# Two elementwise passes of the last node update moved from GpSimd to VectorE

## The chip, the cores and the metric

The kernel runs on one core of a Trainium2 chip. The metric is the device time of one execution in microseconds; three executions of the kernel before are shown, and the middle one is taken. A second, profiled execution gives the trace from which all rows below come. PE is the matrix engine TensorE, DVE the VectorE, ACT the ScalarE, POOL the GpSimd, SP the engine that issues plain transfers.

## The reference

The program is a four-layer graph network on 50000 nodes of 64 channels and 25000 edges. Every layer adds something to the residual `x` and then norms `x` again. The stage that the change touches finishes the third layer. For every node:

```
t = layernorm(h + attended @ Wo' + bias)          (without gain and offset)
y = layernorm(t * g1 + gelu(t @ W1' + b1') @ W2 + bias)
x = x + y * g2 + b2                               (g2, b2: gain and offset of the second norm)
h = relu(layernorm(x));  out starts as x + h
```

`attended` holds one row per edge; the row of a node's last edge is the one that it needs, so it is gathered by an index per node. The last line prepares the fourth layer: its first term is `h`, and `x + h` is written to `out`, to which the later terms are added.

## The kernel before

`node_update(layer 2)` walks over 14 super-tiles. A super-tile is 128 partitions x 28 nodes x 64 channels (a tile of 128x1792 f32 in the profile) and is cut in 7 parts of 4 nodes. Tiles alternate between two buffers each: `A` (gathered rows), `Z` (`h` of before), `T`, `Y`, `TG`, `X` (the residual), `H` (the new `h`). The order on each engine is written out by hand, and they meet through counting semaphores. Super-tile d goes through:

- POOL, `gather` (L1742): 28 indirect DMAs, one per node column, four to a part. Then, when `T` is ready, `gained` (L1722): `TG = T * g1`.
- PE, `attend(d)`: for each part two transposes of `A` (L1327), a bias product (L1333) and two products (L1353). ACT copies the transposes out of PSUM (L1427). The transposes of part i+1 stand ahead of the products of part i. A transposition waits for its part's four gathers; the products of a part wait until DVE has evacuated the part two before.
- PE, `mlp(d)`: turns `T`, two products up (L1368), GELU on ACT (L1433), four products down (L1379). PE's order is attend(d+1), mlp(d), attend(d+2), and so on.
- DVE, `evacuate`: after each part's products it adds PSUM to `Z` (L1554, attend) or to `TG` (L1556, mlp). Between the evacuations it does the norms of up to three super-tiles: during attend(d) the relu and scaling of super-tile d-3 (`H`, L1539) at part 0, the scaling of `T` of d-1 at part 1 (L1540), the centring of `Y` of d-2 at part 2 (L1527) and its variance at part 5 (L1531). During mlp it does the scaling, gain (L1667), sum with the residual (L1671), the totals, centrings and variances. Each of these passes over a whole super-tile.
- ACT also squares the centred rows (L1438) and takes roots (L1442), in a fixed order with its copies.
- POOL, `offset` (L1728): `X = X + b2`, after `X` has been loaded. POOL, `tail` (L1734): `X = X + H`, after `H` is there. It releases SP.
- SP, `swap_x`: waits for the tail, stores `H` and `X`, waits until the store of `X` has landed and loads the next `X` into the same buffer.

POOL's order in the middle of the stage is gathers(d+2), offset(d), gained(d+1), tail(d-1), gathers(d+3): three passes between two sets of gathers. Below, G(d) is the time at which POOL ends the last gather of super-tile d.

Of the kernel before, what the change touches and what calls it, by code (L numbers as in the profile page):

```python
# [1141 lines left out]
def node_update(nc, net, layer, sums=None):  # L1142
# [19 lines left out]
    with ExitStack() as ctx:  # L1162
# [44 lines left out]
        if layer == 2:  # L1207
            Y = [sb(f"y{s}", [P, G, C]) for s in range(2)]
            TG = [sb(f"tg{s}", [P, G, C]) for s in range(2)]
            node_end = sb("node_end", [P, SUPER, G])  # L1210
            ends_loaded = sem("ends_loaded")
            u = [sb(f"u{b}", [FF, 2, CH // 2]) for b in range(2)]

            pf = [ctx.enter_context(nc.psum_tensor(f"{n}pf{b}", [P, 2, 512], F32)) for b in range(2)]
            loaded_x = [sem(f"loaded_x{s}") for s in range(2)]
            gathered = [[sem(f"gathered{s}_{i}") for i in range(SUBS)] for s in range(2)]
            up_done, gelu_done, t_ready, tg_ready, xa_ready, tail_ready = map(
                sem, ("up_done", "gelu_done", "t_ready", "tg_ready", "xa_ready", "tail_ready"))
        weight = (net.w_upd, net.w_lin, net.w_out)[layer]
        x_in = (net.x_in, net.x1, net.x2)[layer]  # L1220
        h_in = (net.h0, net.h1d, net.h2)[layer]
# [21 lines left out]
        with nc.Block() as block:  # L1243
# [268 lines left out]
            def _(v):  # L1512
# [16 lines left out]
                def variance(r, n=0):  # L1529
                    v.wait_ge(squared[n], r + 1)  # L1530
                    nc.vector.tensor_reduce(rstd[n][:, :], SQ[n][:, :, :], AX.X, ALU.add).then_inc(var_ready[n], 1)  # L1531
# [93 lines left out]
                else:  # L1625
                    def attend(c, phase, x=None, t=None, y=None):

                        for i in range(SUBS):
                            if c is not None:
                                if i == 0:  # L1630
                                    v.wait_ge(loaded[c[1]], 16 * in_loads * (c[2] + 1))
                                evacuate(c, phase, i, 0)
                            if x is not None and i == 0:
                                v.wait_ge(stored_h[x[1]], 16 * x[2])
                                nc.vector.tensor_copy(H[x[1]][:, :, C:C + 1], node_end[:, bass.ds(x[0], 1), :].rearrange("p n g -> p g n"))
                                scale(H[x[1]][:, :, 0:C], 2 * x[0] + 1, 1, relu=True).then_inc(normed, 1)
                            elif t is not None and i == 1:
                                scale(T[t[1]][:, :, :], t[0]).then_inc(t_ready, 1)
                            elif y is not None and i == 2:
                                centre(Y[y[1]][:, :, :], 1)  # L1640
                            elif y is not None and i == 5:
                                variance(2 * y[0], 1)
                        v.drain()
                        if c is not None:
                            v.sem_inc(inputs_used, 1)

                    def mlp(c, phase, t=None, y=None):

                        for i in range(SUBS):
                            if c is not None:  # L1650
                                if i == 0:
                                    v.wait_ge(tg_ready, c[0] + 1)
                                evacuate(c, phase, i, 1)
                            if t is not None:
                                if i == 0:
                                    total(T[t[1]][:, :, :])
                                elif i == 1:
                                    centre(T[t[1]][:, :, :])
                                elif i == 3:
                                    variance(t[0])  # L1660
                            if y is not None:
                                xs, ys = X[y[1]][:, :, :], Y[y[1]][:, :, :]
                                if i == 0:
                                    scale(ys, 2 * y[0], 1)
                                elif i == 1:
                                    v.drain()
                                    nc.vector.tensor_tensor(ys, ys, channels(net.norms[:, 2, :]), ALU.mult)  # L1667
                                elif i == 2:
                                    v.drain()
                                    v.wait_ge(xa_ready, y[0] + 1)  # L1670
                                    nc.vector.tensor_tensor(xs, xs, ys, ALU.add)  # L1671
                                elif i == 3:
                                    v.drain()
                                    total(xs, 1)
                                elif i == 4:
                                    centre(xs, 1)
                                elif i == 5:
                                    variance(2 * y[0] + 1, 1)
                        v.drain()
                        if c is not None:  # L1680
                            total(Y[c[1]][:, :, :], 1)
# [19 lines left out]
            @block.gpsimd  # L1701
            def _(pool):
                if layer < 2:
                    with pool.Fori(0, SUPER // 2) as t:
                        for s in range(2):
                            pool.wait_ge(loaded[s], 16 * in_loads * (t + 1))
                            if layer == 0:
                                pool.wait_ge(deg_ready, 2 * t + s + 1)
                                nc.gpsimd.tensor_tensor(Z[s][:, :, C:P], summed(2 * t + s),  # L1709
                                                        inv_count[s][:, :].unsqueeze(2).to_broadcast([P, G, C]), ALU.mult).then_inc(z_ready, 1)  # L1710
                            else:
                                nc.gpsimd.tensor_tensor(A[s][:, :, :], summed(2 * t + s), Z[s][:, :, C:C + 1].to_broadcast([P, G, C]), ALU.mult)
                                pool.drain()
                                nc.gpsimd.tensor_tensor(A[s][:, :, :], A[s][:, :, :], Z[s][:, :, 0:C], ALU.add).then_inc(z_ready, 1)
                else:
                    def channels(which):
                        return net.norms[:, which, :].unsqueeze(1).to_broadcast([P, G, C])

                    def gained(c):

                        pool.wait_ge(t_ready, c[0] + 1)
                        nc.gpsimd.tensor_tensor(TG[c[1]][:, :, :], T[c[1]][:, :, :], channels(0), ALU.mult).then_inc(tg_ready, 1)  # L1722

                    def offset(c):

                        number, s, h = c
                        pool.wait_ge(loaded_x[s], 16 * (h + 1))
                        nc.gpsimd.tensor_tensor(X[s][:, :, :], X[s][:, :, :], channels(3), ALU.add).then_inc(xa_ready, 1)  # L1728

                    def tail(c):  # L1730

                        number, s, h = c
                        pool.wait_ge(normed, number + 1)
                        nc.gpsimd.tensor_tensor(X[s][:, :, :], X[s][:, :, :], H[s][:, :, 0:C], ALU.add).then_inc(tail_ready, 1)  # L1734

                    def gather(c):
                        number, s, h = c
                        if h > 0:
                            pool.wait_ge(inputs_used, number - 1)
                        for j in range(G):  # L1740
                            tile = G * number + j
                            pool.indirect_dma_start(A[s][:, j, :], None, net.attended[:, :],  # L1742
                                                    bass.IndirectOffsetOnAxis(ap=net.dst_end[:, tile:tile + 1], axis=0)).then_inc(gathered[s][j // J], 16)
                    gather(at(0, 0))
                    gather(at(0, 1))
                    for d in range(2):
                        offset(at(0, d))
                        gained(at(0, d))
                        gather(at(0, d + 2))
                    for d in range(2, SUPER):  # L1750
                        gained(at(0, d))
                        tail(at(0, d - 2))
                        if d + 2 < SUPER:
                            gather(at(0, d + 2))
                        offset(at(0, d))
                    tail(at(0, LAST - 1))
                    tail(at(0, LAST))


SET = 4  # L1760
# [844 lines left out]
```

## Time and profile before

| | us |
|---|---|
| median of three executions (5319.16 to 5332.62) | 5328.72 |
| the profiled execution | 5317.69 |
| its span, first to last instruction | 5315.9 |
| the last node update, of that span | 3035 to 3915 |
| busy over the span: PE, DVE, POOL, ACT | 3389.1, 2638.3, 3086.2, 1088.7 |

The engines run side by side, so busy times do not add up to the span. The stages of the program are separated by barriers; a microsecond won inside the last node update is a microsecond of the whole. The busy shares over the span therefore say little about this stage, which is read by stretches of its own.

### The profile page before, as it was taken

What the parts mean: (1) busy time and instruction counts of PE and PEld (TensorE: products, weight loads), DVE (VectorE), ACT (ScalarE), POOL (GpSimd) and SP (SyncE); (2) the same over time, 40 slices, a digit from 0 to 9 for tenths busy, and PEclk for the clock granted to TensorE, in tenths of its full rate; (3) what the DMA queues carried; (4) which work ended last, traced back from release to release, by engine and by line L of the source; (5) the groups of instructions that cost most, each with busy time, mean ns of one, the idle gap of its engine ahead of it and who ended that gap; (6) DMA issues with size and microseconds to landing.
All of it is one profiled execution on the core that took longest, in us unless ns stands there. A gap on an engine that the chain in (4) does not pass through costs nothing. (4 is left out here: it accounts for less than half of the span.)

```text
span 5315.9 us, 58056 instructions
## 1 busy us (share of the span) xinstructions
PE 3389.1 (64%) x12064; PEld 2038.0 (38%) x12064; DVE 2638.3 (50%) x6534; ACT 1088.7 (20%) x2025; POOL 3086.2 (58%) x2552
## 2 busy tenths in 40 slices
PE   3654735555896788676898677776635555555524
PEld 1222534444675666452333244554412222222213
DVE  5997741111355322465666546666644444444423
ACT  0232411111122111122333223332311111111100
POOL 0374048887111881335676588888538888787740
PEclk7686655555555555555555555555557777777765
DMA  3122621111464110451111323333212222233210
GB/s 140 44 71 68 269 102 22 23 23 20 105 166 124 23 22 6 160 203 49 34 34 35 58 42 73 84 86 72 70 43 30 30 30 30 27 30 30 27 16 3
DMA packets 360442, 335.42 MB, mean 63 GB/s; under 512 B 268311, under 2 KB 297481, under 8 KB 360292
## 3 DMA queue, kind: packets, MB, share of 16 engines
q1 hardware_dynamic: 232910, 253.30, 15.1%
q0 software_dynamic: 114032, 67.92, 11.9%
q10 hardware_dynamic: 13350, 12.40, 0.7%
q8 instruction: 69, 1.13, 0.1%
q14 instruction: 81, 0.66, 0.0%
HBM read 172.92 MB, written 162.66 MB: 63 GB/s over the span
## 5 line engine op out<-in xcount | busy, mean ns | idle before, releaser
L843 PE MATMUL e_ps<-e_msg,e_hot 128*128 x2408 | 598.0, 425 | 325.8 <-POOL e_msg L754 231.4
L843 PEld LDWEIGHTS e_ps<-e_msg,e_hot 128*128 128x128 f32 x2408 | 539.4, 326 | 430.5 <-issue 430.5
L2269 POOL DMA_INDIRECT out<-d_out,d_end x356 | 592.0, 1663 | 172.1 <-issue 167.2
L1742 POOL DMA_INDIRECT u_a<-attended,dst_end x392 | 501.0, 1278 | 149.0 <-issue 117.4
L2313 PE MATMUL d_pl<-d_hot,d_fields 128*65 128x512 f32 x712 | 503.1, 872 | 0.0
L815 DVE TENSOR_TENSOR e_ps<-e_ps,e_before 128x65 f32<-128x65 f32 (+1 forms) x172 | 40.1, 233 | 792.5 <-PE e_ps L843 792.5
L2032 POOL DMA_INDIRECT list<-s_rec,s_place x200 | 199.3, 996 | 288.9 <-DVE s_place L1948 232.8
L735 POOL DMA_INDIRECT e_msg<-from_src,e_src x200 | 194.1, 970 | 286.3 <-DMA e_first<-lot_first 231.8
L1427 ACT ACTIVATE u_zt<-u_pt 128x256 f32<-128x256 f32 (+1 forms) x392 | 163.5, 433 | 615.6 <-PE u_pt L1327 615.4
L946 POOL DMA_INDIRECT a_ends<-h,a_src x200 | 201.5, 1007 | 146.7 <-DMA a_etype<-in_etype 93.7
L740 POOL DMA_INDIRECT e_msg<-h1d,e_src x200 | 221.4, 1107 | 102.7 <-issue 54.8
L2294 PE MATMUL d_pc<-d_liveb,d_before 128*128 128x4 bf16 x89 | 14.6, 165 | 387.2 <-DVE d_prod L2411 387.2
L2313 PEld LDWEIGHTS d_pl<-d_hot,d_fields 128*65 128x65 f32 x712 | 140.7, 213 | 292.5 <-issue 292.5
L788 ACT ACTIVATE sums<-e_ps 128x455 f32 (+1 forms) x172 | 94.2, 548 | 748.5 <-DVE e_ps L815 748.5
L737 POOL DMA_INDIRECT e_near<-from_dst,e_dst x200 | 209.4, 1047 | 61.0 <-issue 61.0
L2305 PE MATMUL d_pr<-ident,d_scan 65*128 65x65 f32 x356 | 63.9, 334 | 279.0 <-DVE d_scan L2434 279.0
L1327 PE MATMUL u_pt<-ident,u_a 128*128 128x128 f32 x392 | 118.7, 420 | 191.9 <-DMA u_a<-attended,dst_end 174.4
L946 POOL DMA_INDIRECT a_ends<-h,a_dst x200 | 202.2, 1011 | 66.6 <-issue 66.0
L2261 POOL DMA_INDIRECT d_near<-term,d_rec x196 | 189.9, 969 | 85.1 <-issue 71.1
L1709 POOL TENSOR_TENSOR u_z<-sums,u_inv_count 128x1792 f32<-128x1792 f32 x14 | 44.6, 3189 | 306.7 <-DVE u_inv_count L1563 261.2
L1333 PE MATMUL u_po<-bias_parts,ones 3*128 3x256 bf16 x392 | 149.8, 382 | 111.9 <-ACT u_zt L1427 80.5
L2261 POOL DMA_INDIRECT d_near<-terms,d_rec_idx x168 | 163.5, 973 | 98.5 <-DMA d_rec_w<-list_w 49.8
(370 smaller groups left out, 7910.4 us busy)
## 6 DMA issues: line engine op xcount, KB each, us to landing
u_z<-h SPq DMA_DIRECT2D x28, 896.0 KB, 6.3
x<-sums SPq DMA_DIRECT2D x28, 896.0 KB, 7.8
u_x<-x SPq DMA_DIRECT2D x28, 896.0 KB, 7.4
terms<-s_zeros SPq DMA_DIRECT2D x16, 812.5 KB
s_key_row<-src_key SPq DMA_DIRECT2D x50, 256.0 KB, 3.0
h1d<-u_h SPq DMA_DIRECT2D x14, 910.0 KB, 9.5
u_z<-h1d SPq DMA_DIRECT2D x14, 910.0 KB, 4.6
term<-u_h SPq DMA_DIRECT2D x14, 910.0 KB, 3.6
```

The lines of the kernel that those rows point to most:

```text
L735: pool.indirect_dma_start(msg[:, b, 0:C], None, net.from_src[:, :], bass.IndirectOffsetOnAxis(ap=src[:, b:b + 1], axis=0)).then_inc(gather ...
L737: pool.indirect_dma_start(near[c % 3][:, j, :], None, net.from_dst[:, :], bass.IndirectOffsetOnAxis(ap=dst[:, b:b + 1], axis=0)).then_inc( ...
L740: pool.indirect_dma_start(msg[:, b, :], None, net.h1d[:, :], bass.IndirectOffsetOnAxis(ap=src[:, b:b + 1], axis=0)).then_inc(gathered[c % ...
L843: last = nc.tensor.matmul(to, hot[s][:, q, :], rows, start=False, stop=q == LOT - 1)
L946: pool.indirect_dma_start(ends[s][:, j, half * C:(half + 1) * C], None, net.h2[:, :], bass.IndirectOffsetOnAxis(ap=rows, axis=0)).then_inc ...
L1333: nc.tensor.matmul(po[b][:, 0:J * C], net.ones3[:, :], net.bias_parts[:, which, :, :].rearrange("k j c -> k (j c)"), start=True, stop=False)
L1427: nc.scalar.activation(zt[b][:, :], pt[b][:, 0:TURNS * P], ACT.Copy).then_inc(zt_ready, 1)
L1742: pool.indirect_dma_start(A[s][:, j, :], None, net.attended[:, :], bass.IndirectOffsetOnAxis(ap=net.dst_end[:, tile:tile + 1], axis=0)).th ...
L2032: pool.indirect_dma_start(net.lists0[:, :], bass.IndirectOffsetOnAxis(ap=place[:, t:t + 1], axis=0), rec[:, t, :], None).then_inc(scattere ...
L2261: pool.indirect_dma_start(near[s][:, j, :], None, table[:, :], bass.IndirectOffsetOnAxis(ap=row, axis=0)).then_inc(gathered[s], 16)
L2269: pool.indirect_dma_start(net.out[:, :], bass.IndirectOffsetOnAxis(ap=end[s][:, j:j + 1], axis=0), out[s][:, j, 0:C], None, bounds_check=N ...
L2313: last = nc.tensor.matmul(pl[0:WEIGHT + 1, :], fields[:, j, :], hot[:, j, :], start=j == 0, stop=j == J - 1)
```

## The change

`X + b2` and `X + H` are issued by DVE in `attend` instead of by POOL. The first stands behind the evacuation of part 3 and belongs to super-tile d-2; it waits for the load of `X`, and what follows on DVE waits with it. The second stands behind the evacuation of part 4, belongs to super-tile d-3, and has a drain ahead of it; it sends the signal for SP's stores. POOL's `offset` and `tail` go with the semaphore between them and the sum with the residual, so that POOL's order becomes gathers(d+2), gained(d+1), gathers(d+3). Nothing else of the program differs.

```diff
--- before.py
+++ after.py
@@ -1214,8 +1214,8 @@
             pf = [ctx.enter_context(nc.psum_tensor(f"{n}pf{b}", [P, 2, 512], F32)) for b in range(2)]
             loaded_x = [sem(f"loaded_x{s}") for s in range(2)]
             gathered = [[sem(f"gathered{s}_{i}") for i in range(SUBS)] for s in range(2)]
-            up_done, gelu_done, t_ready, tg_ready, xa_ready, tail_ready = map(
-                sem, ("up_done", "gelu_done", "t_ready", "tg_ready", "xa_ready", "tail_ready"))
+            up_done, gelu_done, t_ready, tg_ready, tail_ready = map(
+                sem, ("up_done", "gelu_done", "t_ready", "tg_ready", "tail_ready"))
         weight = (net.w_upd, net.w_lin, net.w_out)[layer]
         x_in = (net.x_in, net.x1, net.x2)[layer]
         h_in = (net.h0, net.h1d, net.h2)[layer]
@@ -1640,6 +1640,12 @@
                                 centre(Y[y[1]][:, :, :], 1)
                             elif y is not None and i == 5:
                                 variance(2 * y[0], 1)
+                            if y is not None and i == 3:
+                                v.wait_ge(loaded_x[y[1]], 16 * (y[2] + 1))
+                                nc.vector.tensor_tensor(X[y[1]][:, :, :], X[y[1]][:, :, :], channels(net.norms[:, 3, :]), ALU.add)
+                            elif x is not None and i == 4:
+                                v.drain()
+                                nc.vector.tensor_tensor(X[x[1]][:, :, :], X[x[1]][:, :, :], H[x[1]][:, :, 0:C], ALU.add).then_inc(tail_ready, 1)
                         v.drain()
                         if c is not None:
                             v.sem_inc(inputs_used, 1)
@@ -1667,7 +1673,6 @@
                                     nc.vector.tensor_tensor(ys, ys, channels(net.norms[:, 2, :]), ALU.mult)
                                 elif i == 2:
                                     v.drain()
-                                    v.wait_ge(xa_ready, y[0] + 1)
                                     nc.vector.tensor_tensor(xs, xs, ys, ALU.add)
                                 elif i == 3:
                                     v.drain()
@@ -1721,18 +1726,6 @@
                         pool.wait_ge(t_ready, c[0] + 1)
                         nc.gpsimd.tensor_tensor(TG[c[1]][:, :, :], T[c[1]][:, :, :], channels(0), ALU.mult).then_inc(tg_ready, 1)
 
-                    def offset(c):
-
-                        number, s, h = c
-                        pool.wait_ge(loaded_x[s], 16 * (h + 1))
-                        nc.gpsimd.tensor_tensor(X[s][:, :, :], X[s][:, :, :], channels(3), ALU.add).then_inc(xa_ready, 1)
-
-                    def tail(c):
-
-                        number, s, h = c
-                        pool.wait_ge(normed, number + 1)
-                        nc.gpsimd.tensor_tensor(X[s][:, :, :], X[s][:, :, :], H[s][:, :, 0:C], ALU.add).then_inc(tail_ready, 1)
-
                     def gather(c):
                         number, s, h = c
                         if h > 0:
@@ -1743,18 +1736,10 @@
                                                     bass.IndirectOffsetOnAxis(ap=net.dst_end[:, tile:tile + 1], axis=0)).then_inc(gathered[s][j // J], 16)
                     gather(at(0, 0))
                     gather(at(0, 1))
-                    for d in range(2):
-                        offset(at(0, d))
+                    for d in range(SUPER):
                         gained(at(0, d))
-                        gather(at(0, d + 2))
-                    for d in range(2, SUPER):
-                        gained(at(0, d))
-                        tail(at(0, d - 2))
                         if d + 2 < SUPER:
                             gather(at(0, d + 2))
-                        offset(at(0, d))
-                    tail(at(0, LAST - 1))
-                    tail(at(0, LAST))
 
 
 SET = 4

```

## Rows read from the trace of the kernel before

**Rows 1.** Windows of the last node update: lead-in, one early period, nine periods, drain.
```profile
...
core 0: us, PE busy (x) PEld busy (x) DVE busy (x) ACT busy (x) POOL busy (x), PEclk, DMA share, GB/s
3035.00:3155.70 120.70, 67.29 (x240) 44.59 (x240) 32.35 (x41) 23.89 (x42) 95.52 (x87) 0.50 0.43 70
...
3209.50:3263.30 53.80, 41.26 (x154) 28.53 (x154) 35.11 (x35) 17.55 (x29) 45.40 (x31) 0.50 0.39 86
3263.30:3780.40 517.10, 373.44 (x1386) 256.36 (x1386) 315.91 (x315) 158.13 (x261) 441.45 (x281) 0.50 0.36 78
3780.40:3915.40 135.00, 58.67 (x222) 40.59 (x222) 89.80 (x64) 30.94 (x46) 34.42 (x9) 0.50 0.18 69
...
```

**Rows 2.** Waits of PE, POOL, SP from 3324 to 3738 us: total, times, longest.
```profile
...
PE u_pt L1327 <- DMA u_a<-attended,dst_end: 75.6, 21, 6.1
...
POOL u_a L1742 <- issue: 59.5, 199, 0.3
...
SPq L1254 <- DMA out<-u_x: 46.0, 7, 7.0
...
```

**Rows 3.** Timeline of POOL, one period; start, duration, operation, idle before.
```profile
...
3435.80 3.97 POOL L1728 TENSOR_TENSOR u_x<-u_x,norms 128x1792 f32<-128x1792 f32 x1
...
3447.45 0.97 POOL L1742 DMA_INDIRECT u_a<-attended,dst_end  x1 [0.16 <-issue]
...
3453.86 2.62 POOL L1742 DMA_INDIRECT u_a<-attended,dst_end  x1 [0.31 <-issue]
3456.78 1.81 POOL L1742 DMA_INDIRECT u_a<-attended,dst_end  x1 [0.30 <-issue]
...
3462.59 0.94 POOL L1742 DMA_INDIRECT u_a<-attended,dst_end  x1 [0.30 <-issue]
...
3492.20 0.94 POOL L1742 DMA_INDIRECT u_a<-attended,dst_end  x1 [0.30 <-issue]
...
```

**Rows 4.** Groups by line, 3324 to 3738 us: POOL's gathers and two passes, mean ns.
```profile
...
L1742 POOL DMA_INDIRECT u_a<-attended,dst_end x199 | 265.6, 1335 | 59.5 <-issue 59.5
...
L1728 POOL TENSOR_TENSOR u_x<-u_x,norms 128x1792 f32<-128x1792 f32 x8 | 31.8, 3973 | 0.1
...
L1734 POOL TENSOR_TENSOR u_x<-u_x,u_h 128x1792 f32<-128x1792 f32 x8 | 29.3, 3658 | 0.0
...
```

**Rows 5.** Timeline of DVE, the same period.
```profile
...
3453.63 2.03 DVE L1527 TENSOR_TENSOR u_xc<-u_t,u_mean 128x1792 f32<-128x1792 f32 x1
3455.75 2.03 DVE L1667 TENSOR_TENSOR u_y<-u_y,norms 128x1792 f32<-128x1792 f32 x1
...
3462.24 2.01 DVE L1531 TENSOR_REDUCE u_rstd<-u_sq 128x28 f32<-128x1792 f32 x1
...
3484.76 0.42 DVE L1554 TENSOR_TENSOR u_t<-u_po,u_z 128x256 f32<-128x256 f32 x1
3492.46 0.42 DVE L1554 TENSOR_TENSOR u_t<-u_po,u_z 128x256 f32<-128x256 f32 x1 [7.28 <-PE u_po L1353]
```

**Rows 6.** Timeline of PE, the same period: two transposes that follow the gathers.
```profile
...
3437.81 0.66 PE L1327 MATMUL u_pt<-ident,u_a 128*128 128x128 f32 x2 [2.69 <-DMA u_a<-attended,dst_end]
...
3490.29 0.66 PE L1327 MATMUL u_pt<-ident,u_a 128*128 128x128 f32 x2 [6.10 <-DMA u_a<-attended,dst_end]
...
```

**Rows 7.** Timeline of DVE in the drain.
```profile
...
3803.22 5.29 DVE L1671 TENSOR_TENSOR u_x<-u_x,u_y 128x1792 f32<-128x1792 f32 x1
...
3831.78 5.37 DVE L1527 TENSOR_TENSOR u_xc<-u_y,u_mean 128x1792 f32<-128x1792 f32 x1
3838.91 2.02 DVE L1531 TENSOR_REDUCE u_rstd<-u_sq 128x28 f32<-128x1792 f32 x1 [1.76 <-ACT u_sq L1438]
...
```

**Rows 8.** Timeline of POOL in the drain.
```profile
...
3802.48 4.14 POOL L1728 TENSOR_TENSOR u_x<-u_x,norms 128x1792 f32<-128x1792 f32 x1 [10.61 <-DMA u_x<-x]
...
3902.99 3.64 POOL L1734 TENSOR_TENSOR u_x<-u_x,u_h 128x1792 f32<-128x1792 f32 x1 [24.13 <-DVE u_h L1539]
```

**Rows 9.** DMA issues on the page: size and us to landing.
```profile
...
u_x<-x SPq DMA_DIRECT2D x28, 896.0 KB, 7.4
...
```

## The prediction

> **What bounds the kernel now.** I first cut the stage into windows [rows 1]. From 3263.3 to 3780.4 us it repeats nine times with a period of 517.1/9 = 57.5 us; the period before those takes 53.8 us, since POOL makes only two passes in it. PE is busy for 373.4/9 = 41.5 us of a period and DVE for 35.1 us; neither is full. Next come the waits [rows 2]: POOL never waits for another engine, only "issue" stands ahead of its gathers (0.30 us each), so POOL is full. PE waits for gathers 75.6 us in 414 us, which is 10.5 us per period. So POOL's chain sets the period, and PE, with its other waits in, would need 57.5 - 10.5 = 47.0 us. The granted clock is 0.50 (1.2 GHz) in every window, and PE's own speed does not matter as long as it waits for gathers.
>
> The timeline of POOL [rows 3] shows what fills it. Call G the end of the last gather: 3435.8, and again 3492.20 + 0.94 = 3493.14. From G three passes take 11.65 us (to 3447.45), and then 28 gathers follow. A gather takes 0.94 us plus 0.30, but the mean is 1.335 us [rows 4]: (1.335 - 0.944) x 28 = 10.9 us per period is stretch. The timeline of DVE [rows 5] tells where it comes from. A pass with two inputs in SBUF starts at 3453.63 and ends at 3455.66; the gather of 3453.86 ends at 3456.48, 0.82 us later [rows 3]. The next such pass (3455.75 to 3457.78) catches the gather of 3456.78 for its last microsecond and it takes 1.81 us. The reduction of 3462.24, one input, leaves the gather of 3462.59 at 0.94. Eight gathers of a period are stretched, and DVE makes eight passes with two SBUF inputs in gather time. My rule for the sum: a gather that starts while such a pass runs ends 0.82 us after the pass. Replayed over the eight passes it gives 11.65 + 34.7 + 11.0 = 57.4 us, the measured period.
>
> **The change, part by part.** *Taken off POOL:* 3.97 us and 3.66 us per period [rows 4]. On the chain one pass of 4.1 us (with 0.16 us of issue) stays of 11.65: -7.6 us per period.
>
> *Put on DVE, first pass (`X + b2`).* It has the shape and kind of the passes in [rows 5], so it takes 2.03 us. It stands behind the evacuation of part 3, which starts at 3484.76, 49.0 us behind G [rows 5]; the pass runs from +49.5 to +51.5. PE's place relative to G stays as it is: its last transposition of `A` starts 2.0 us behind G, when that gather has landed [rows 6], and from there to part 3 of the next attend it did not depend on how late POOL was. The pass lies in gather time, so it stretches a gather. Bounds: 0.87 us (the 1.81 us gather) and 2.03 us (the whole pass). By the rule it catches the 28th gather, which ends at 51.53 + 0.82 = 52.35 instead of 51.1: +1.2 us.
>
> *Second pass (`X + H`), 2.03 us.* The evacuation of part 4 starts at 3492.46 and ends at 3492.88 [rows 5], 2.2 us behind the transposition of 3490.29 that followed a gather [rows 6], and 0.26 us ahead of G. With a drain the pass starts just ahead of G, and `gained`, which now starts right behind G, meets it. What happens when POOL's and DVE's passes meet is seen in the drain: DVE's pass of 3803.22 takes 5.29 us, because POOL's had started at 3802.48 [rows 7, 8]; the second to come waits out the first. Here POOL loses the rest of DVE's pass, 1.8 us. If POOL is first, DVE waits 4 us and then catches the first gather, for about as much. Bounds again 0.87 and 2.03; I take 1.8. What is queued behind either pass on DVE is the evacuation of parts 4 and 5, and PE waits for those. The cover is the 7.28 us that DVE idles ahead of part 4 [rows 5] and the 10.5 us of PE; without cover it is 4.1 us of DVE time per period.
>
> *Sum of a period.* The eight old passes fall on other gathers by this shift and cost 10.6 instead of 11.0. From G: 4.1 + 1.8 + 34.7 + 10.6 + 1.2 = 52.4 us, -5.1 us.
>
> *SP.* The signal for the stores now comes near G and not three passes later; the store of `X` holds SP up to 7.0 us [rows 2], the load lands in 7.4 us [rows 9], and the first pass wants it some 49 us on. Cost nothing; if that cover went, DVE would stand in the wait with all evacuations behind it. The removed semaphore costs nothing.
>
> *Lead-in.* Up to G(3), POOL loses two passes `X + b2` (-7.9). The first one on DVE comes behind a G that is now 4 us earlier, so it waits for `gained` and catches a gather (+1.9), the other stretches one (+1.3): -4.7 us.
>
> *From G(3) to G(13).* One period 53.8 to 52.4, -1.4; nine from 57.5 to 52.4, 517.1 - 9 x 52.35 = -45.9.
>
> *Drain.* The 5.29 us pass no longer meets POOL's: 3.3 us of DVE, of which PE sees between none and all; I take 1.3, since DVE has idle time behind it. The pass of 3831.78 (5.37) loses 3.3 us behind POOL's `X + H`; now two passes of 2.1 us stand behind it instead, but the 1.76 us wait for ACT's square [rows 7] is hidden by them: -0.9. The same shape once more for the last super-tile: -1.0. The very last pass, 3.64 us on POOL [rows 8], becomes a drain and 2.03 on DVE: -1.6. Together -4.8.
>
> Sum: -4.7 - 1.4 - 45.9 - 4.8 = **-57 us**. Against the profiled execution (5317.7) this is 5261; the median of the runs shown is 11 us above that execution, and I predict for it 5328.7 - 57 = 5272.
>
> The stretched gather is where row and notes part. The Trainium skill (SBUF — State Buffer, "Who interferes with whom") says that a DVE instruction with two SBUF inputs contends only with a GpSimd instruction that reads SBUF, and adds as an inference that such a pass did not stall DMAs whose descriptors GpSimd makes. Taken to the letter the two passes would cost POOL nothing, which is the second case below. The trace speaks against it by the gather of 2.62 us [rows 3].
>
> **The rivals.** *POOL is relieved in full.* The added passes fall where they catch no gather and no pass. Period 57.5 - 7.6 = 49.9 us, still above PE's 47.0; 9 x 7.6 + 3.9 + 7.9 + 4.8 = -85, 5244 us. Against it: eight of eight such passes are stretched for now. Chance 0.07.
>
> *DVE and PE take over.* In attend the evacuations of parts 0 to 3 already have passes between them, and now parts 3 and 4 too. If the `X + H` pass always loses to `gained` and waits its 3.97 us, and all of this reaches PE, its loop is 47.0 + 4.1 + 4.0 = 55.1 us. Gain 2.4 us in nine periods, a loss of 1.3 in the early one, lead-in and drain as above: about -30, 5299 us. For it: the 5.37 us pass [rows 7]. Against it: the idle 7.28 us just there. Chance 0.14.
>
> *Nothing left.* Catches of 2.03 us at both passes and an attend that is slower than I see, 57 us per period: within 16 us of before. Chance 0.05.
>
> *Slower: both passes lose the port.* The place is attend, parts 3 to 5; each pass waits 3.97 us for a pass of POOL, and PE waits for both: 47.0 + 2 x (2.03 + 3.97) = 59.0 us, +1.5 in nine periods and +5.2 in the early one: some +19, 5348 us. It decides once more than 10.5 us reach PE in a period. Against it: only one POOL pass is left per period for the two to meet. Chance 0.03.
>
> That the passes are not moved at all is excluded by the diff.
>
> **How the numbers follow.** My forecast has 0.71: 5272, with both added passes at 0.87 us (period about 51.2) 5261, with both at 2.03 us (about 53.5) 5283; executions differ by some 7 us around that. The measurement can tell about 0.3%, 16 us, from no change. Range for 8 in 10: 5252 to 5293; it reaches toward the full relief and toward the takeover by DVE, without holding either. Faster by over 0.3%: 0.71 + 0.07 + 0.14 = 0.92, taken down to 0.91; within: 0.06; slower: 0.03.
>
> **What would show it.** Right: windows of the same nine periods sum to about 471 us; POOL still waits for nobody; ten gathers or passes of POOL are stretched per period, one of them `gained` with nearly 5.8 us instead of 3.97; the gathers' mean in a period stays near 1.36 us; PE's wait for gathers falls to some 5 us per period; DVE is busy for 39 us of 52. The DVE passes in attend take 2.03 us. Wrong: POOL waits for `T` or for used inputs (then PE or DVE sets the period), the `X + H` pass takes 5 to 6 us and PE waits for evacuations, or the gathers' mean falls to what eight passes make.

## The result and the profile after

Five executions of the changed kernel have a median of 5279.1 us (5256.0 to 5281.7), five of the kernel before 5320.4 us. The ratio is 0.991, with an interval of 0.9893 to 0.9926: 48 us gained (39 to 57). The two medians differ by 41.3 us; the changed kernel's executions lie in two groups, 5256 to 5259 and 5279 to 5282 us. The forecast was 5272 us, -57.

The profiled execution, the fastest of the five, took 5256.0 us with a span of 5254.2, which is 61.7 us less than before. Not all of that is the change. The last node update starts its first gather at 3018.39 us instead of 3034.83, though no code ahead of it differs, and the stage behind it is 4.8 us longer. The stage itself, from its first gather to the first instruction of the next, takes 834.7 us instead of 884.7: **-50.0 us**. In what follows I compare this stage, whose steady periods repeat within 0.2 us, and not the whole.

Windows of the changed kernel, cut at G(3), G(4) and G(13) as in [rows 1], and last a window of one period:

```profile
...
core 0: us, PE busy (x) PEld busy (x) DVE busy (x) ACT busy (x) POOL busy (x), PEclk, DMA share, GB/s
3018.39:3186.60 168.21, 103.84 (x394) 70.11 (x394) 69.21 (x77) 40.66 (x71) 134.64 (x114) 0.52 0.38 62
3186.60:3237.67 51.07, 39.83 (x151) 27.72 (x151) 40.46 (x35) 16.70 (x29) 42.67 (x30) 0.50 0.42 90
3237.67:3708.45 470.78, 354.79 (x1366) 247.94 (x1367) 375.39 (x329) 157.13 (x259) 358.37 (x261) 0.53 0.40 86
3708.45:3853.10 144.65, 65.09 (x247) 45.25 (x246) 102.72 (x81) 33.68 (x50) 7.92 (x2) 0.50 0.17 64
3448.96:3501.77 52.81, 39.61 (x153) 27.93 (x154) 42.20 (x38) 17.17 (x28) 39.82 (x29) 0.53 0.41 87
...
```

The nine periods sum to 470.8 us; 471 was forecast. DVE has 375.4 us in them instead of 315.9, POOL 358.4 instead of 441.5: POOL is no longer full. The waits, over the eight last periods, from 3290.52 to 3713.04 us (line waited for, total, times, longest):

```profile
...
PE u_po L1333 <- issue: 40.8, 11, 5.1
PE u_pf L1368 <- ACT u_zt L1427: 35.8, 16, 2.7
PE u_po L1333 <- ACT u_u L1433: 18.3, 8, 2.3
PE u_po L1333 <- DVE u_t L1554: 6.0, 8, 0.8
...
```

```profile
...
POOL u_a L1735 <- issue: 66.0, 217, 0.3
POOL u_tg L1727 <- DVE u_t L1540: 37.0, 8, 4.6
```

PE's wait for gathers [rows 2] is gone altogether. POOL now waits for `T` once per period, 4.6 us each. PE's largest wait is put down to "issue", up to 5.1 us. Its cause is in the timelines. POOL's, of one period:

```profile
...
3443.40 0.94 POOL L1735 DMA_INDIRECT u_a<-attended,dst_end  x1 [0.30 <-issue]
3448.96 3.96 POOL L1727 TENSOR_TENSOR u_tg<-u_t,norms 128x1792 f32<-128x1792 f32 x1 [4.62 <-DVE u_t L1540]
3453.07 0.97 POOL L1735 DMA_INDIRECT u_a<-attended,dst_end  x1
3454.34 1.61 POOL L1735 DMA_INDIRECT u_a<-attended,dst_end  x1 [0.30 <-issue]
3456.26 1.95 POOL L1735 DMA_INDIRECT u_a<-attended,dst_end  x1 [0.31 <-issue]
3458.51 2.14 POOL L1735 DMA_INDIRECT u_a<-attended,dst_end  x1 [0.30 <-issue]
```

The gathers of a super-tile end at 3444.34 and POOL stands until `T` is scaled. DVE's timeline around it:

```profile
...
3446.85 2.03 DVE L1540 TENSOR_TENSOR u_t<-u_xc,u_rstd 128x1792 f32<-128x1792 f32 x1
3448.79 0.42 DVE L1554 TENSOR_TENSOR u_t<-u_po,u_z 128x256 f32<-128x256 f32 x1
3449.30 3.65 DVE L1525 TENSOR_SCALAR u_mean<-u_mean 128x28 f32<-128x28 f32 x1
3453.03 2.10 DVE L1527 TENSOR_TENSOR u_xc<-u_y,u_mean 128x1792 f32<-128x1792 f32 x1
3455.05 0.41 DVE L1554 TENSOR_TENSOR u_t<-u_po,u_z 128x256 f32<-128x256 f32 x1
3455.38 2.01 DVE L1645 TENSOR_TENSOR u_x<-u_x,norms 128x1792 f32<-128x1792 f32 x1
...
3457.81 2.03 DVE L1648 TENSOR_TENSOR u_x<-u_x,u_h 128x1792 f32<-128x1792 f32 x1
...
3467.82 0.42 DVE L1556 TENSOR_TENSOR u_y<-u_po,u_tg 128x256 f32<-128x256 f32 x1 [5.39 <-PE u_po L1379]
...
3499.66 2.03 DVE L1540 TENSOR_TENSOR u_t<-u_xc,u_rstd 128x1792 f32<-128x1792 f32 x1
...
```

The scaling of `T` ends at 3448.88 and POOL's pass starts at 3448.96. On DVE the evacuation of part 2 goes through in its usual 0.42 us, and behind it comes a scaling of 28 means per partition, which took 0.18 to 0.39 us in the periods before. It takes 3.65 us now: it stands until POOL's pass ends at 3452.92. From 3446.85 to 3460 DVE has no gap. From one scaling of `T` to the next it is 3499.66 - 3446.85 = 52.81 us, against 57.5 before. PE feels it:

```profile
...
3444.01 1.22 PE L1353 MATMUL u_po<-w_out,u_zt 128*128 128x128 f32 x4
...
3446.86 0.71 PE L1353 MATMUL u_po<-w_out,u_zt 128*128 128x128 f32 x4
...
3455.56 0.37 PE L1333 MATMUL u_po<-bias_parts,ones 3*128 3x256 bf16 x1 [5.12 <-issue]
...
3457.82 0.37 PE L1333 MATMUL u_po<-bias_parts,ones 3*128 3x256 bf16 x1 [0.75 <-DVE u_t L1554]
...
3462.87 2.08 PE L1368 MATMUL u_pf<-u_zt,w 64*128 64x256 f32 x8 [2.67 <-ACT u_zt L1427]
...
```

PE's products of part 5 start at 3455.56, when DVE has evacuated part 3 at 3455.46; the wait of 5.12 us is DVE's lateness. The wait of 2.67 us at the start of mlp has the same source, by way of ACT:

```profile
...
3462.13 0.32 ACT L1442 ACTIVATE u_rstd<-u_rstd,eps 128x28 f32<-128x28 f32 x1 [5.01 <-DVE u_rstd L1531]
3462.36 0.64 ACT L1427 ACTIVATE u_zt<-u_pt 128x256 f32<-128x256 f32 x2
...
```

In ACT's fixed order the root of `Y`'s variance stands ahead of the copies of `T`'s transposes, and it waits for the variance that DVE makes behind part 5.

In the drain, the pass that took 5.29 us [rows 7] is down to 2.03, the means' scaling stands behind POOL's pass as it did before the change, and the last pass of the stage is on DVE with 2.02 us instead of 3.64 [rows 8]:

```profile
...
3741.77 2.03 DVE L1676 TENSOR_TENSOR u_x<-u_x,u_y 128x1792 f32<-128x1792 f32 x1
...
3764.78 3.98 DVE L1525 TENSOR_SCALAR u_mean<-u_mean 128x28 f32<-128x28 f32 x1
...
3837.51 2.02 DVE L1648 TENSOR_TENSOR u_x<-u_x,u_h 128x1792 f32<-128x1792 f32 x1
...
```

### The profile page after: what moved, and what is told of

It reads as the page before. It is cut to its first block and busy times, and to the rows that moved or that the text cites. A ratio compares the mean times of both kernels' runs of the same rounds, so it can differ in the third digit from the quotient of the medians.

```text
span 5254.2 us, 58073 instructions
## 1 busy us (share of the span) xinstructions
PE 3366.0 (64%) x12064; PEld 2026.4 (39%) x12064; DVE 2716.5 (52%) x6562; ACT 1088.7 (21%) x2025; POOL 2973.1 (57%) x2524
## 5 line engine op out<-in xcount | busy, mean ns | idle before, releaser
L1735 POOL DMA_INDIRECT u_a<-attended,dst_end x392 | 488.1, 1245 | 149.5 <-issue 116.3
L2393 DVE SCALAR_TENSOR_TENSOR d_live<-d_near,d_inside 128x4 f32<-128x4 f32 x89 | 14.5, 163 | 392.0 <-DMA d_near<-term,d_rec 222.5
```

## Experiments

The period below is from one scaling of `T` to the next in the middle of the stage; the stage runs from its first gather to the first instruction of the next stage; the time is of the profiled execution, or a median where several were timed. A single time is not compared below; the period is.

| kernel | period, us | POOL's wait for T per period | stage, us | time, us |
|---|---|---|---|---|
| before | 57.44 | none | 884.7 | 5320.4 |
| the change | 52.82 | 4.62 | 834.7 | 5279.1 |
| gain_behind_4_gathers | 52.2 | none | 823.8 | 5265.1 |
| gain_on_dve | 49.52 | (no pass on POOL) | 790.5 | 5239.2 |
| gain_on_dve_again | 49.52 | (no pass on POOL) | 786.5 | 5239.7 |
| only_b2_on_dve | 55.40 | none | 865.3 | 5303.7 |
| no_x_passes | 49.9 | none | 794.5 | 5227.1 |
| before_plus_two_input_pass | 58.45 | none | 898.8 | 5319.2 |
| before_plus_reduction | 57.44 | none | 884.4 | 5310.5 |
| after_plus_reduction | 54.75 | 5.87 | 857.2 | 5285.7 |
| b2_behind_part_6 | 51.0 | 2.0 | disturbed | 5426.9 |
| x_h_only_on_dve | 56.0 to 56.9 | 5.12 | disturbed | 5464.9 |
| gain_on_dve_b2_behind_part_6 | 47.6 | (no pass on POOL) | disturbed | 5427.1 |
| gain_b2_part_6_again | 47.5 to 50.0, mean 48.9 | (no pass on POOL) | 776.6 | 5224.1 |

The three marked as disturbed ran on a chip on which the kernel before took 5682 us; only their steady periods are used.

**What does a DVE pass cost POOL?** The kernel before, with one more operation behind part 3 of attend:

```diff
                                 evacuate(c, phase, i, 0)
+                                if i == 3:
+                                    nc.vector.tensor_tensor(spare[:, :, :], Z[c[1]][:, :, :], channels(net.norms[:, 3, :]), ALU.add)
```

> The kernel before, with one more DVE pass of two SBUF inputs (Z + b2 into a buffer that nobody reads) behind the evacuation of part 3 of attend. Theory: POOL sets the period, the pass stretches one gather and nothing else, +0.9 to +2.0 us on 57.4 us, 1.2 us by the rule (a caught gather ends 0.82 us after the pass), so 58.6 us. Rival, a DVE pass costs nothing while POOL is the bound, since the gathers' long ones come from elsewhere: 57.4 us.

and with `nc.vector.tensor_reduce(spare[:, :, 0], Z[c[1]][:, :, :], AX.X, ALU.add)` in its place:

> The kernel before, with a DVE reduction over Z (one SBUF input, 2.0 us) in the same place. Theory: a pass with one input doesn't stretch a gather, 57.4 us. Rival, any DVE pass of 2 us stretches a gather: 58.6 us as with two inputs.

The groups of gathers on the two pages, first with two inputs, then with the reduction:

```profile
...
L1745 POOL DMA_INDIRECT u_a<-attended,dst_end x392 | 514.9, 1314 | 147.6 <-issue 117.4
...
```

```profile
...
L1745 POOL DMA_INDIRECT u_a<-attended,dst_end x392 | 500.6, 1277 | 149.4 <-issue 117.4
...
```

Two inputs: 58.45 us, +1.0; the mean gather is longer by 0.037 us, which times 28 is the same 1.0. The reduction: 57.44 us, nothing. The stretched gather is shown: while POOL is full, a DVE pass with two SBUF inputs costs its period 1.0 us at this place (1.2 by my rule), and this reduction with a single input is free.

**Who sets the period of the changed kernel?** The same reduction, free for POOL, in the changed kernel:

> The changed kernel with the same reduction of 2.0 us (one input, which by the theory costs POOL nothing) behind part 3 of attend. Theory: in the changed kernel DVE's chain through attend sets the period, so the 2.0 us are seen in full: 52.8 to 54.8 us, stage 834.7 + 9 x 2 = 853 us. Rival, POOL's gathers set it: 52.8 us, 834 us.

The period rises from 52.82 to 54.75 us, by nearly all of its 2.0 us, and POOL waits 5.87 us for `T` instead of 4.62; its gathers take up the other 0.7 us (waits of POOL, 3290 to 3690 us):

```profile
...
POOL u_tg L1730 <- DVE u_t L1541: 47.0, 8, 5.9
```

So DVE's chain through attend sets the period, not POOL.

**Is the blocked scaling part of it?** POOL's pass with `g1` behind the first gathers of the next super-tile:

```diff
                     for d in range(SUPER):
+                        if d + 2 < SUPER:
+                            gather(at(0, d + 2), 0, 4)
                         gained(at(0, d))
                         if d + 2 < SUPER:
-                            gather(at(0, d + 2))
+                            gather(at(0, d + 2), 4, G)
```

> The changed kernel, but POOL issues the first four gathers of the next super-tile ahead of its pass with g1. The stage is counted from its first gather to the first instruction of the next stage: 884.7 us before, 834.7 us with the change. Theory: a loop through attend on DVE and PE now sets the period of 52.8 us, and 3.3 us of it is the small scaling of Y's mean, which waits behind POOL's pass because both start when T is ready. With the pass behind four gathers the scaling should take 0.4 us again, the loop 49.4 us, and POOL (34.7 us of gathers, 4.1 us for its pass, ten stretched gathers of 1.2 us) sets the period at 50.8 to 51.5 us: stage 820 to 825 us. Rival 1: POOL's gathers set the period as before and the wait for T is only slack; then the order on POOL changes nothing, 834 us. Rival 2: the added passes on DVE alone set it; then the scaling may be short but the period stays 52.8 us.

Groups by line and the wait of PE for gathers, 3290 to 3680 us:

```profile
...
L1735 POOL DMA_INDIRECT u_a<-attended,dst_end x211 | 300.5, 1424 | 63.3 <-issue 63.3
...
L1525 DVE TENSOR_SCALAR u_mean<-u_mean 128x28 f32<-128x28 f32 x22 | 7.1, 325 | 2.1
...
```

```profile
...
PE u_pt L1327 <- DMA u_a<-attended,dst_end: 49.1, 8, 6.6
...
```

The means' scaling is back at a mean of 0.33 us (its three uses in a period of the changed kernel take 3.65, 0.39 and 0.18 us), PE waits for gathers again, and POOL waits for nobody. POOL took over at 52.2 us, above the 51.5 that I had stated, since ten catches cost (1.424 - 0.944) x 28 = 13.4 us and not the 12 that I had put in. The block is gone, and the period gains little because POOL, full again, needs 52.2 us. In the whole time the gain cannot be told from the change's: a ratio of 0.9906 (0.9887 to 0.9924) to before. How long DVE's loop is without the block had to be seen where POOL has no pass at all:

```diff
+                            if t is not None and i == 6:
+                                nc.vector.tensor_tensor(TG[t[1]][:, :, :], T[t[1]][:, :, :], channels(net.norms[:, 0, :]), ALU.mult).then_inc(tg_ready, 1)
```

```diff
                     for d in range(SUPER):
-                        gained(at(0, d))
                         if d + 2 < SUPER:
```

> The changed kernel with the last pass of POOL (T times g1) on DVE too, behind part 6 of attend, so that POOL has gathers alone. Theory: the loop through DVE loses the 3.3 us wait and gains a pass of 2.03 us, 52.8 - 3.3 + 2.0 = 51.5 us a period at most, less where DVE was idle there (5.4 us ahead of part 0 of mlp): 49.5 to 51.5 us, stage 805 to 823 us. Rival, POOL's gathers set the period: 34.7 us + 11 stretched gathers of 1.2 us = 48 us, stage about 790 us. Rival, DVE's total work sets it: 2 us more of it, stage 850 us or more.

Timeline of DVE, and the waits of PE over eight periods:

```profile
...
3447.26 0.39 DVE L1525 TENSOR_SCALAR u_mean<-u_mean 128x28 f32<-128x28 f32 x1
...
3456.97 2.02 DVE L1644 TENSOR_TENSOR u_tg<-u_t,norms 128x1792 f32<-128x1792 f32 x1
3462.45 0.42 DVE L1556 TENSOR_TENSOR u_y<-u_po,u_tg 128x256 f32<-128x256 f32 x1 [3.46 <-PE u_po L1379]
...
```

```profile
...
PE u_pf L1368 <- ACT u_zt L1427: 36.1, 16, 2.7
PE u_po L1333 <- ACT u_u L1433: 16.0, 7, 2.3
PE u_po L1333 <- issue: 7.0, 8, 0.9
...
```

The scaling takes 0.39 us, the added pass lies in the idle time ahead of mlp's part 0, and the period is 49.52 us: 52.82 less the 3.3 us of the block. POOL makes its 28 gathers in 48.27 us, less than the period, so it does not set it. That is the lower end of the theory's 49.5 to 51.5, and of the rivals none; the stage of 790 us missed the theory's 805 to 823 and is what I had written under the POOL rival, since lead-in and drain became shorter too.

Five more executions of the same kernel:

> The kernel gain_on_dve once more, timed: its stage was 790.5 us against 884.7 before and 834.7 with the change. The first run took 5239.2 us. Expected: 5225 to 5245 us, 1.5 to 1.8% below before.

The ratio to before is 0.9849 (0.9831 to 0.9867).

**One half at a time.** `X + H` back on POOL behind `gained`, `X + b2` on DVE:

```diff
                         gained(at(0, d))
+                        if d >= 2:
+                            tail(at(0, d - 2))
                         if d + 2 < SUPER:
```

> Half of the change: X + b2 on DVE, X + H stays on POOL behind its pass with g1. Theory: POOL sets the period again: 34.7 us of gathers, 7.9 us of passes, nine stretched gathers of 1.2 to 1.37 us, so 53.4 to 55 us, stage 840 to 858 us; POOL waits for nothing. The rule of the prediction gives 57.4 - 3.97 + 1.2 = 54.7 us. Rival, the loop through DVE sets it here too: 52.8 - 2.3 = 50.5 us, stage 815 us.

55.40 us, against 54.7 by the rule and 53.4 to 55 stated, and a stage of 865.3 us against 840 to 858: POOL is full as expected, and my price for the stretches was low. The other half, `X + b2` on POOL behind the gathers as before, `X + H` on DVE:

```diff
                         gained(at(0, d))
                         if d + 2 < SUPER:
                             gather(at(0, d + 2))
+                        if d >= 2:
+                            offset(at(0, d))
```

> The other half of the change: X + H on DVE, X + b2 on POOL. The half with X + b2 on DVE gave 55.4 us. Theory: POOL sets the period, with 7.9 us of passes and nine or ten catches: 54.5 to 56.0 us, stage 850 to 868 us. Rival, DVE's chain sets it, with one pass less than in the changed kernel: 50.5 us.

56.0 to 56.9 us, at and above the upper edge of 54.5 to 56.0, and not for the stated reason. POOL waits 5.1 us per period for `T`, and two small operations of DVE are blocked (DVE, then POOL, one period):

```profile
...
3470.78 3.44 DVE L1635 COPY u_h<-u_node_end 128x28 f32 x1
...
3479.64 3.65 DVE L1525 TENSOR_SCALAR u_mean<-u_mean 128x28 f32<-128x28 f32 x1
...
```

```profile
...
3470.18 3.98 POOL L1731 TENSOR_TENSOR u_x<-u_x,norms 128x1792 f32<-128x1792 f32 x1
3479.28 3.96 POOL L1725 TENSOR_TENSOR u_tg<-u_t,norms 128x1792 f32<-128x1792 f32 x1 [5.12 <-DVE u_t L1540]
...
```

This ran on the disturbed chip; whether the rest of the period is its lateness stays open.

Neither pass, on any engine:

```diff
-                                nc.vector.tensor_tensor(X[y[1]][:, :, :], X[y[1]][:, :, :], channels(net.norms[:, 3, :]), ALU.add)
...
-                                nc.vector.tensor_tensor(X[x[1]][:, :, :], X[x[1]][:, :, :], H[x[1]][:, :, 0:C], ALU.add).then_inc(tail_ready, 1)
+                                v.sem_inc(tail_ready, 1)
```

> The changed kernel without X + b2 and X + H, so that out misses b2 and h and what follows from x lacks b2; all waits and signals stay. Theory: the loop through DVE and PE is 4.5 us shorter (two passes and their gaps), 48.3 us, and POOL with 34.7 + 4.1 + eight stretched gathers of 1.37 = 49.7 us sets the period; DVE's scaling of the mean no longer meets POOL's pass, since POOL comes later than T. Stage about 800 us. Rival, the loop is PE's alone and the added passes lie in its shadow: 52.8 us as with the change, 834 us.

49.9 us with POOL full (49.7 was expected from 34.7 + 4.1 + 8 stretches). The kernel leaves out `b2` and `h`, so its output is not the program's. POOL's one pass and its gathers, with the eight old stretches, thus already need 49.9 us.

**Is the place on DVE what counts?** In the changed kernel:

```diff
-                            if y is not None and i == 3:
+                            if y is not None and i == 6:
                                 v.wait_ge(loaded_x[y[1]], 16 * (y[2] + 1))
```

> The changed kernel, with X + b2 on DVE behind part 6 of attend instead of part 3, where DVE idles 5.4 us ahead of mlp's part 0. Theory: the pass leaves DVE's chain through attend, 2.26 us with its gap, so the loop takes 52.8 - 2.3 = 50.5 us; POOL by itself needs 48.2 to 50.5 us; period 50.5 to 51.5 us, stage 814 to 823 us. Rival, DVE's total work or the number of stretched gathers sets the period: 52.8 us and 834 us, as its place doesn't change them.

51.0 us, as expected: 1.8 less than with the same work at part 3, so neither DVE's total work nor the number of stretched gathers (nine now, eight in the changed kernel) sets the period. The same edit on top of gain_on_dve:

> gain_on_dve (all three passes on DVE, loop 49.5 us, stage 786 to 790 us), with X + b2 behind part 6, beside T times g1. DVE idled 3.5 us there, so the pass of 2.0 us is covered. Theory: the loop through DVE falls by 2.3 us to 47.3 us and POOL's gathers, 48.3 us in that kernel, set the period at 47.5 to 48.5 us: stage 775 to 782 us, time 5220 to 5232 us. Rival, the loop isn't shorter because PE, not DVE, needs 49.5 us: stage 786 to 790 us.

DVE's loop is 47.6 us, as expected (47.3). And on a chip where before takes 5322 us:

> gain_on_dve_b2_behind_part_6 once more, since in its call the kernel before itself took 5682 us instead of 5318. Its loop through DVE took 47.6 us there. Where the kernel before takes about 5318 us: theory, POOL's gathers set the period at 47.5 to 48.5 us, stage 775 to 782 us, time 5220 to 5232 us; rival, the gain over gain_on_dve (5239.7 us) is hidden by POOL's gathers, 5235 to 5242 us.

Stage 776.6 us, median 5224.1 us, ratio 0.9818 (0.9791 to 0.9844). The period changes between 47.5 and 50.0 us with a mean of 48.9, a little above the 47.5 to 48.5 expected; PE waits for gathers again, so POOL's gathers hold it up. Stage and time fell in their ranges. It is the fastest kernel of the study, 55 us below the changed one.

## Why the prediction came out as it did

**What bounded the kernel before:** right. The added reduction costs nothing there, the added pass only what it stretches.

**The passes taken off POOL and the stretched gathers:** right in kind, 1.0 us measured where the rule gave 1.2. The Trainium skill (SBUF — State Buffer, "Who interferes with whom") says that a DVE instruction with two SBUF inputs contends with a GpSimd instruction that reads SBUF, and infers that a `tensor_tensor` leaves descriptor generation alone. The inference does not hold for these gathers: two inputs +1.0 us, one input 0. The first half does not speak against them as I had read it, since a gather takes its indices from a tile in SBUF (`net.dst_end`); whether it is this read that is held, no run shows.

**The step that failed** is "The cover is the 7.28 us that DVE idles ahead of part 4 [rows 5] and the 10.5 us of PE". With it the sum of a period took nothing for DVE and kept POOL's terms alone. Both waits were there only because POOL was late, and the change takes away just that: by the prediction's own numbers a period of 52.4 us leaves PE 52.4 - 47.0 = 5.4 us and not 10.5. In the way of it stand the two passes, some 1.9 us each (52.8 against 51.0, and 49.5 against 47.6, when `X + b2` goes behind part 6; for `X + H` the same is assumed), and 3.3 us that the sum did not have at all, those for which the means' scaling stands behind `gained`: 7.1 us together. DVE now has no gap from part 0 to part 6 of attend, and the loop takes 52.8 us. Without the block it takes 49.5 (gain_on_dve), less than the 52.2 us at which POOL is full in gain_behind_4_gathers; so it is the block that hands the period from POOL to DVE. The 47.0 itself was not too low: 49.5 less two passes of 1.9 us is 45.7 us, an estimate, since POOL is full at 49.9 us in no_x_passes.

The block could have been read from the trace before. In its drain, where POOL comes early as it does now, the scaling of `T` releases `gained` (first row, POOL) and the means' scaling (second row, DVE) at once:

```profile
...
3827.71 3.96 POOL L1722 TENSOR_TENSOR u_tg<-u_t,norms 128x1792 f32<-128x1792 f32 x1 [21.09 <-DVE u_t L1540]
...
```

```profile
...
3827.73 3.98 DVE L1525 TENSOR_SCALAR u_mean<-u_mean 128x28 f32<-128x28 f32 x1
...
```

The prediction read the row right below, the pass of 5.37 us [rows 7], and passed over this one.

**What the second pass meets:** wrong. I put 1.8 us for `X + H` meeting `gained` at G. It meets nothing there: POOL came early, `gained` starts when `T` is ready, and what stands right behind that on DVE is the centring of `Y`, 3.3 us late. This is my rival "DVE and PE take over" in mechanism, at another place (part 2, not part 4) and with 52.8 us instead of 55.1. I had given it 0.14.

**The signs.** Of what was to show the forecast wrong, "POOL waits for `T`" came true. Of what was to show it right, the nine periods (470.8 us for 471) and the length of DVE's passes in attend (2.01 and 2.03 us) did, and the rest did not: eight gathers of a period are stretched and not ten, `gained` takes 3.96 us and not 5.8, the gathers' mean is 1.28 us and not 1.36, PE does not wait for gathers, and DVE is busy for 41.7 us of 52.3. Two slips of the working changed nothing: the full relief is the first rival and not the "second case", and the sum of the slower rival leaves out the -9.5 us of lead-in and drain that the others have, so that it would be +9 and not +19.

**Why the number was near all the same.** By luck. Term by term, forecast and measured: lead-in -4.7 and -6.5; the early period -1.4 and -2.7; nine periods -45.9 and -46.3; drain -4.8 and +5.4; sum -56.8 and -50.0. The nine periods agree by accident: one of 48.2 us, which is POOL's own chain with eight catches, and eight of 52.8, which is DVE's; average 52.3. The forecast's 52.4 was POOL's chain with ten catches and a meeting that did not take place. The drain's +5.4 is a matter of the cut: POOL now ends G(13) far ahead of PE. From the evacuation of part 0 in the last but one mlp to the next stage it is 121.2 us instead of 126.3, -5.0, next to the -4.8 of the forecast; its terms were not measured one by one. The whole time moved by 48 us (39 to 57), an interval that holds the stage's 50 and reaches the forecast's 57 at its edge.

**Shown and not shown.** Shown: who sets the period (the reduction), the 3.3 us of the block (two edits take the scaling back to 0.39 us, and the one that also frees POOL brings the loop to 49.52 us), the cover ahead of mlp (b2_behind_part_6, by its periods on the disturbed chip). Argued only: that POOL came early in the first place because the lead-in has fewer passes than the middle. Open: why the half with `X + H` is slower than the sum of its stretches.

## What to carry to other kernels

A wait for the bounding engine hides work on every other engine in the same loop. Before relieving the bound, replay the loop of the others with that wait at zero and the new work in it, each operation in its order, and count as cover only what the new period leaves (here 5.4 us), not the wait of the old one (10.5 us). Where two engines block each other, look at what each issues when the same signal releases both: here 28 elements on DVE cost 3.65 us because POOL's pass started on the same event. Work moved onto an in-order engine belongs where that engine idles ahead of a wait, not in the stretch that others wait for: moving `X + b2` from part 3 to part 6 took 1.8 us off the period.

## What the runs showed of the hardware

A scaling or a copy on DVE over 28 elements per partition is held until a POOL pass that is under way ends: 3.65 us for the scaling and 3.44 us for the copy, where 0.39 and 0.18 are usual. A reduction and an evacuation out of PSUM were not held: while POOL's three passes of the kernel before ran (3435.80 to 3447.29), they took 2.01 us (3440.32) and 0.41 us (3442.25). A POOL gather that starts while a DVE pass with two SBUF inputs runs took up to 2.72 us instead of 0.94, and beside a reduction 0.94.

In the changed kernel the granted clock of a period is 0.53 instead of 0.50: four products of a part take 0.71 us at the higher level (2.4 GHz) where 1.22 is usual (3446.86 against 3444.01). From the first product of mlp on PE had worked with no gap over 2.3 us. It fell back behind the waits of attend. That it was worth nothing is argued: PE stood waiting for DVE there.
